# Attention between two expert layers: the sine product moved from GpSimd to VectorE, and the steps from row sums to division moved one period apart

## The reference

```
c_q, c_kv = h @ w_down_q.T, h @ w_down_kv.T          # h is the layer-normed x, latent width 128
q = rope(c_q @ w_up_q.T); k = rope(c_kv @ w_up_k.T); v = c_kv @ w_up_v.T      # 16 heads of 64
rot = stack([e * cos - o * sin, e * sin + o * cos])  # e, o: even and odd columns of a head
attn = softmax(q @ k.T / 8);  out = (attn @ v) @ w_out.T + x
```

## Time and profile before

| what | value |
|---|---|
| runs | 4849.31 us median of 3 (4834.95 to 4853.02) |
| profiled execution | 4841.01 us, span 4839.2 us |
| attention, by first and last QL (L961) | 581.7 to 4208.5 us, 64 heads |
| PE busy | 4281.5 us, 88% of the span |
| DVE, POOL, ACT busy | 3247.4, 3223.5, 2114.6 us |

### The profile page before, as it was taken

One profiled execution on the slowest core, in us unless ns is written; L12 is line 12 of the kernel. 1 busy time (PEld: TensorE's weight loads), 2 busy tenths in 40 slices (PEclk: granted clock), 3 DMA queues, 4 the chain that ended last, 5 costly groups with the idle time before them and its releaser, 6 DMA issues. The chain is left out here.

```text
span 4839.2 us, 69491 instructions
## 1 busy us (share of the span) xinstructions
PE 4281.5 (88%) x27328; PEld 2584.2 (53%) x27328; DVE 3247.4 (67%) x3875; ACT 2114.6 (44%) x2776; POOL 3223.5 (67%) x1602
## 2 busy tenths in 40 slices
PE   7999688998898889988998898889889988969999
PEld 6888444444444444444444444444444444438888
DVE  6555477777767776777677767767776777735554
ACT  4444244444344444444444444444434444424444
POOL 3444377777777777777777777867777777734444
PEclk9999799999999999999999999999999999979999
DMA  3332200001000100010011001000100011022332
GB/s 129 103 106 96 78 23 27 27 27 51 27 30 29 45 29 27 27 45 27 27 42 34 28 30 45 29 26 30 45 27 27 27 36 42 25 71 88 102 101 90
DMA packets 162934, 233.18 MB, mean 48 GB/s; under 512 B 37454, under 2 KB 87344, under 8 KB 161968
## 3 DMA queue, kind: packets, MB, share of 16 engines
q1 hardware_dynamic: 162608, 228.74, 14.7%
HBM read 134.81 MB, written 26.21 MB: 33 GB/s over the span
## 5 line engine op out<-in xcount | busy, mean ns | idle before, releaser
L1042 POOL TENSOR_TENSOR atACC<-atACC,atPT 128x1024 f32<-128x1024 f32 x768 | 1909.6, 2486 | 129.8 <-ACT atPT L900 63.8
L966 DVE TENSOR_REDUCE atNM<-atPS 128x2 f32<-128x1024 f32 x1024 | 1204.1, 1217 | 853.8 <-PE atPS L789 851.2
L900 ACT ACTIVATE atPT<-atPS 128x1024 f32<-128x1024 f32 x1024 | 999.8, 1024 | 637.8 <-PE atPS L815 618.5
L825 PE MATMUL atPO<-atPT,atV 128*64 128x512 f32 x4096 | 971.5, 595 | 0.0
L1028 POOL TENSOR_TENSOR atVT<-atVT,atSIN 128x512 f32<-128x512 f32 x256 | 351.8, 1374 | 713.5 <-DMA atVT<-atR 713.1
L815 PE MATMUL atPS<-atQH,atKL 64*128 64x512 f32 x2048 | 486.0, 465 | 100.2 <-ACT atSH L891 99.9
L825 PEld LDWEIGHTS atPO<-atPT,atV 128*64 128x64 f32 x4096 | 283.9, 137 | 471.6 <-issue 461.2
L789 PE MATMUL atPS<-atKH,atQH 64*128 64x512 f32 x2048 | 451.1, 452 | 18.8 <-ACT atPT L900 12.0
L815 PEld LDWEIGHTS atPS<-atQH,atKL 64*128 64x128 f32 x2048 | 211.5, 195 | 432.2 <-issue 409.8
L815 PE MATMUL atPS<-atQL,atKH 64*128 64x512 f32 x2048 | 435.4, 413 | 0.0
L815 PE MATMUL atPS<-atQH,atKH 64*128 64x512 f32 x2048 | 434.9, 412 | 0.0
(11 more groups left out here) (244 smaller groups left out, 7358.6 us busy)
## 6 DMA issues: line engine op xcount, KB each, us to landing
atVT<-atR SPq DMA_DIRECT2D x512, 128.0 KB, 2.0
f1GB<-f1GD SPq DMA_DIRECT2D x128, 256.0 KB, 6.6
atRSUM<-atRD SPq DMA_DIRECT2D x128, 256.0 KB, 3.9
f2GB<-f2GD SPq DMA_DIRECT2D x128, 256.0 KB, 6.9
x<-X SPq DMA_DIRECT2D x7, 1024.0 KB, 4.5
X<-x SPq DMA_DIRECT2D x7, 1024.0 KB, 5.5
f1XB<-in_x SPq DMA_DIRECT2D x5, 1024.0 KB, 5.7
x<-f1XB SPq DMA_DIRECT2D x5, 1024.0 KB, 8.2
```

Source lines behind the costliest of these rows:

```text
L825: ins = pe.eng.matmul(PO[HI[h], :], V[n % 2][:, j, HI[h]], PT[k % NPT][:, h, :], start=j == 0, stop=j == T - 1)
L900: act.eng.activation(PT[k % NPT][:, :, :], PS[ring.of[step]][:, :, :], ACT.Exp, scale=SCALE).then_inc(grown.sem)
L966: dve.eng.tensor_reduce(NM[:, q, t, :], PS[ring.of[step]][:, :, :], AX.X, ALU.max, negate=True).then_inc(most_out.sem)
L1042: pool.eng.tensor_tensor(ACC[t][:, :, :], begun[:, :, :], PT[k % NPT][:, :, :], ALU.add).then_inc(gathered.sem)
```

## The change

The rotation's sine product is issued by DVE directly ahead of the sum, and both stand late in the period after the one in which the sum stood. `invert`, `inverse`, `broadcast` and `divide` each have a period of their own (3, 4, 5, 6 in place of 2, 3, 3, 5), with two RSUM buffers. PE waits for SH ahead of the fourth product of a score in place of the first. The halves' maximum is taken by a reduce of pairs in place of a product of two tensors.

```diff
-            RSUM, RQ = sb("RSUM", [128, S], fp32), sb("RQ", [128, 16], fp32)
+            RSUM, RQ = [sb(f"RSUM{i}", [128, S], fp32) for i in range(2)], sb("RQ", [128, 16], fp32)
...
                     at(early, m, k - 4, ("raise", m, i, t))
-                    at(begin, m, k - 3, ("sine", m, i, t))
-                    at(end, m, k - 3, ("rotate", m, i, t))
+                    at(late, m, k - 2, ("rotate", m, i, t))
...
-                at(end, m, 18, ("invert", m))
-                at(end, m, 19, ("inverse", m), ("broadcast", m))
-                at(end, m, 21, ("divide", m, 0), ("divide", m, 1))
+                at(end, m, 19, ("invert", m))
+                at(end, m, 20, ("inverse", m))
+                at(end, m, 21, ("broadcast", m))
+                at(end, m, 22, ("divide", m, 0), ("divide", m, 1))
...
-                        pe.wait_ge(*row_out(n, t))
...
                             q = qq[n % 2] if qq else SH
+                            if k == 3:
+                                pe.wait_ge(*row_out(n, t))
...
-                        act.wait_ge(*divided.past(n - 1, t))
+                        act.wait_ge(*divided.past(n - 2, t))
...
                         k, before = swap_of(n, i, t)
+                        dve.wait_ge(*swapped[k](n, i, t))
+                        dve.eng.tensor_tensor(VT[k][:, :], VT[k][:, :], SIN[:, sl], ALU.mult).then_inc(sined.sem)
                         dve.wait_ge(*sined(n, i, t))
...
-                        dve.eng.tensor_tensor(MF[:, some, :], NM[:, some, 0, :], NM[:, some, 1, :], ALU.min).then_inc(minus.sem)
+                        dve.eng.tensor_reduce(MF[:, some, :], NM[:, some, :, :], AX.X, ALU.min, negate=False).then_inc(minus.sem)
...
-                    elif name == "sine":
-                        _, n, i, t = step
-                        k, before = swap_of(n, i, t)
-                        pool.wait_ge(*ups(3))
-                        pool.wait_ge(*swapped[k](n, i, t))
-                        pool.eng.tensor_tensor(VT[k][:, :], VT[k][:, :], SIN[:, t * 512:(t + 1) * 512], ALU.mult).then_inc(sined.sem)
```

More of the change, by code:

```diff
@@ L910, in scalar @@
                         act.wait_ge(*summed(n, t))
-                        act.wait_ge(*divided.past(n - 1, t))
-                        act.eng.activation(RSUM[:, t * 512:(t + 1) * 512], OT[:, :], ACT.Copy).then_inc(sum_out.sem)
+                        act.wait_ge(*divided.past(n - 2, t))
+                        act.eng.activation(RSUM[n % 2][:, t * 512:(t + 1) * 512], OT[:, :], ACT.Copy).then_inc(sum_out.sem)
             def vector(dve):
@@ L965, in vector @@
                         dve.wait_ge(*minus.past(n - 1, q // 4))
-                        dve.eng.tensor_reduce(NM[:, q, t, :], PS[ring.of[step]][:, :, :], AX.X, ALU.max, negate=True).then_inc(most_out.sem)
+                        dve.eng.tensor_reduce(NM[:, q, :, t], PS[ring.of[step]][:, :, :], AX.X, ALU.max, negate=True).then_inc(most_out.sem)
                     elif name == "minus":
@@ L986, in vector @@
                         dve.wait_ge(*attend_out(n, t))
-                        dve.eng.tensor_tensor(o, o, RSUM[:, t * 512:(t + 1) * 512], ALU.mult).then_inc(divided.sem)
+                        dve.eng.tensor_tensor(o, o, RSUM[n % 2][:, t * 512:(t + 1) * 512], ALU.mult).then_inc(divided.sem)
                     elif name == "outward":
@@ L1069, in sync @@
                         for h in range(2):
-                            line = RSUM[64 * h:64 * h + 1, :].rearrange("o (p i) -> o p i", i=16)
+                            line = RSUM[n % 2][64 * h:64 * h + 1, :].rearrange("o (p i) -> o p i", i=16)
                             sp.eng.dma_start(RQ[HI[h], :], line).then_inc(columns.sem, 16)
@@ L1082, in sync @@
                         for h in range(2):
-                            sp.eng.dma_start(RSUM[HI[h], :], RD[n % 2][h:h + 1, :].broadcast_to([64, S])).then_inc(broadcast.sem, 16)
+                            sp.eng.dma_start(RSUM[n % 2][HI[h], :], RD[n % 2][h:h + 1, :].broadcast_to([64, S])).then_inc(broadcast.sem, 16)
                     elif name == "outward":
```

## The result

The changed kernel takes 5129.78 us (median of 4 runs, 5124.32 to 5133.04) against 4842.13 before (4 runs, 4821.0 to 4853.02): a ratio of 1.060, 95% interval 1.0575 to 1.0618. The forecast was 5095 in a range of 4700 to 5200. Its profiled execution took 5132.47 us (span 5130.7), so 291.5 us of span are to be found.

A forecast was written before the change was run, and what follows sets the result against it. PE was taken to bound the attention, waiting for DVE's lateness in periods 6 and 7. The terms summed to +4.0 us a head, +256 us in 64 heads, about 5097 us, stated as 5095; 8-in-10 range 4700 to 5200.

The forecast's parts named there:

- the signs named: Profile after: idle ahead of `sum` under 60 us, `row` 250 or more, mosts 250 or more, SH wait under 20.
- (a): PE's wait for SH, moved behind three of four products of a score: -1.4 us a head.
- (b): Between period 5's cosine product and period 6's mosts, divisions and a rotate go, with PE's `sum` wait: -3.5 us a head.
- (c): Period 6 to 7: six contending DVE instructions meet POOL's sums, PE's row waits 6.0 us: +4.4, taken as +3.2 a head.
- My discount: On the row's wait in period 7: one POOL block less in half of the heads, -1.2 us, +4.4 to +3.2.
- (d): Third rotate late, so ACT's copy to KH delays period 1's exponentials and PE's second most: +2.0 us a head.
- (e): Fourth rotate late, blocked by POOL, so QH's copy delays period 2's exponential: +3.8 even, +2.5 odd heads, mean 3.1.
- (g): PE's lower clock after waits: by proportion up to 3.1 us, taken as 2.2 since 2 us waits leave little: +0.6 a head.
- The rival of POOL's gaps: DVE finds gaps between POOL's sums, one block instead of three in period 6 to 7: 154 us faster, 4690; chance 0.22.

The follow-up runs named there:

- the run with shorter sums: Changed kernel with POOL adding only the first of two heads' 512 columns in sums 2 to 7 of each half (wrong results, timing only): 4573.34 us, ratio 0.946.

## Why the prediction was right, and where it was lucky

The direction and the mechanism hold by intervention: moving the steps that wait for the rotation, and the divisions that stand ahead of the minus, takes 535 of 5130 us away, and halving most of what blocks DVE takes 556. Of the signs named, one failed by a little: the idle time ahead of `sum` fell to 68.2 us and not under 60.

(a) -1.4 us a head: -1.36 measured. (b) -3.5: sum idle fell by 154 us, so -2.4. The heads whose layer norm stands at the end of period 5 (in one of them four instructions of L939 took 7.61 us together, beside POOL's sums) kept a wait of 4.8 to 5.1 us there, where I had let all of them go. (c) The row's wait was worked out as 6.0 and is 5.3 in an undisturbed head; over all heads the group grew by 152 us, +2.4 where I had taken +3.2. My discount, one block less in half of the heads, went in the right direction for a wrong reason: no block is missing in most heads; in two of eight the row doesn't wait at all, because the sum does.

(d) is right: 123.6 us of waits in period 1 are 1.9 a head, where +2.0 was taken. (e) took +3.1 and the waits in period 2 are 134.0 us, 2.1 a head. In the even head the two blocks of (e) are there, but PE was late too, by then, since it had run at the lower clock after KH's wait; so it stood 1.98 us and not 3.8. In the odd head I had the outward hold DVE, as it does, but with POOL in the way behind it, which it is not; PE stands 1.86 us of the 2.5. As length of periods 1 and 2 the two are +6.2.

(g) is the term that was mis-sized. The aftermath was taken as +0.6 a head; it is +2.3, PE's 149.7 us of more busy time. The premise of the discount, that waits of 2 us leave little, is what failed: of the 119 waits of 1.1 to 2.4 us ahead of the mosts in periods 1 and 2, 34 were followed by 4 us at the full clock and 85 by 4 us at 0.57 to 0.65 in the mean. The kernel before had it to be seen: after the 27 waits of over 2 us ahead of `row` (2.7 in the mean) the next 4 us ran at 0.67 in the mean. The granted clock of 0.60 in the earlier trace rows was also read too mildly: with levels of 1 and 0.5 it is four fifths of the stretch at the lower one, not half.

The sum came out near, +4.0 against 4.55, by luck in part: its idle time was +3.4 where 2.2 was measured, over-counted in (c) and (e) and under-counted in (b), and the aftermath was under-counted by 1.7. A period's length is the quantity to work out; its idle part alone can't be.

The rival of POOL's gaps fell: three of six instructions were blocked in the head shown, and the row waits 5.3 us in six heads of eight. The rule of the Trainium skill on the shared port (SBUF — State Buffer, Who interferes with whom) holds here as the rows show it, blocks of up to 2.2 us while a sum of POOL's ran, and none where POOL's sums were over, as in the rows of the run with shorter sums. The same section says that a reduce on trn2 never contends; the trace agrees for the pair-minimum: 0.15 us beside POOL's sums, and at most 0.17 in all 128. What I left out of the rivals was a part of the place: not only where the rotation stands, but which copies wait for it. What the reduce of pairs is worth by itself no run here shows. The changed kernel with two groups of its table moved is 5% faster than the kernel before, as changed it is 6% slower.

## What to carry to other kernels

When a step moves one slot later, list who waits for it and what stands behind them in their queues: here ACT's copy of KH, one microsecond long, held the exponentials, and these held PE's PSUM bank. Where two engines block each other for whole instructions, a small one can take as long as the other's large one (the bf16 copy of 8 columns: 2.13 us against 0.18 at least), so count the contending instructions between a result and its reader, not their own time. And judge a wait by the length of the stretch around it, since an engine that stood still can come back slower.

## What the hardware showed that I had not expected

The lower clock follows short waits too, but not all of them. Windows of PE in the changed kernel (start:end, length, PE busy, clock, DMA share, GB/s):

```profile
2109.00:2111.30 2.30, 0.52 (x6) 1.00 0.00 0
2111.30:2115.00 3.70, 3.63 (x24) 0.62 0.02 4
2118.00:2120.50 2.50, 0.55 (x6) 1.00 0.00 0
2120.50:2124.00 3.50, 3.46 (x28) 1.00 0.00 0
2158.00:2162.00 4.00, 4.00 (x24) 0.50 0.18 66
```

After a wait of 1.85 us (the window 2109.00:2111.30) the next 3.7 us ran at a mean of 0.62; after one of 1.98 us (2118.00:2120.50) the next 3.5 us ran at 1.00; after the 5.29 us one (ahead of 2158.00) it was 0.50 for 4 us, the lower of the two levels (1.2 GHz). Length alone doesn't decide: over the kernel, waits of 1.85 to 1.92 us stand on both sides. No run here tells what does.
